# Expert slots cut into four quarters of 32 rows instead of two halves of 64

## The reference

```python
scores = sigmoid(x @ gate_w)                       # 1024 x 32 experts, in 4 groups
...                                                # two groups are barred, six experts per token are kept
g = ragged_dot(xs, w_gate, group_sizes)            # xs: 6144 rows (1024 tokens x 6), sorted by expert
u = ragged_dot(xs, w_up, group_sizes)              # w_gate, w_up: 32 x 256 x 176
d = ragged_dot(silu(g) * u, w_down, group_sizes)   # w_down: 32 x 176 x 256
expert_out = sum(d[unsort_idx].reshape(T, 6, 256) * weights[..., None], axis=1)
shared = (silu(x @ sw_gate) * (x @ sw_up)) @ sw_down
```

## Time and profile before

| | |
|---|---|
| median of 3 runs | 800.51 us (800.24 to 805.26) |
| the profiled execution | 803.87 us |
| its span on the core | 802.10 us, so 1.77 us lie around it |
| TensorE's granted clock, mean | 0.949 of full speed |

### The profile page before, as it was taken

The page is one execution under the profiler, slowest core; times in us unless marked ns, Lnnn a source line. Parts: engine busy times, 40 slices in busy tenths (PEclk is TensorE's granted clock), DMA queues, the critical chain, the costliest instruction groups (busy, mean ns, idle before and its releaser), DMA issues. The chain is left out here.

```text
span 802.1 us, 17814 instructions
## 1 busy us (share of the span) xinstructions
PE 712.0 (89%) x6749; PEld 447.1 (56%) x6749; DVE 447.9 (56%) x1151; ACT 305.7 (38%) x668; POOL 205.3 (26%) x263
## 2 busy tenths in 40 slices
PE   4999978876889999999999998699699999999945
PEld 3777755644344454665656775477445555555534
DVE  2567658876368887565645554259723443434426
ACT  1233334354310102444444443233255656556440
POOL 4000110143200000000000000024447777777422
PEclk9999999999779999999999999579879999999979
DMA  9500000000295000000000000195023232232157
GB/s 260 160 2 2 2 2 2 2 3 3 102 301 190 1 1 1 2 2 1 2 2 2 2 3 2 45 309 132 10 70 98 95 97 96 92 101 92 62 175 230
DMA packets 47544, 55.24 MB, mean 69 GB/s; under 512 B 6918, under 2 KB 42598, under 8 KB 46758
## 3 DMA queue, kind: packets, MB, share of 16 engines
q1 hardware_dynamic: 40390, 36.86, 15.8%
q0 software_dynamic: 6656, 16.85, 6.6%
q10 hardware_dynamic: 416, 0.39, 0.2%
HBM read 41.45 MB, written 12.65 MB: 67 GB/s over the span
## 5 line engine op out<-in xcount | busy, mean ns | idle before, releaser
L680 ACT ACTIVATE pt<-bank 128x512 f32<-128x512 f32 x192 | 104.2, 595 | 201.1 <-PE bank L390 112.8
L378 PE MATMUL bank<-kk,qT 32*128 32x256 f32 x768 | 109.6, 402 | 12.3 <-DVE qs L836 9.6
L836 DVE TENSOR_REDUCE qs<-bank 128x4 f32<-128x512 f32 x128 | 82.3, 684 | 54.9 <-PE bank L378 54.8
L1123 POOL TENSOR_TENSOR rstd<-vare,half 128x1 f32<-128x1 f32 x32 | 18.4, 574 | 348.6 <-DVE vare L899 348.6
L378 PEld LDWEIGHTS bank<-kk,qT 32*128 32x128 f32 x768 | 67.4, 185 | 38.1 <-issue 28.8
L1599 PE MATMUL bank<-x_wgu,x_xgT 128*64 128x352 f32 x256 | 84.8, 476 | 0.0
L1599 PE MATMUL bank<-wgu,x_xgT 128*64 x256 | 84.8, 475 | 0.0
L390 PE MATMUL bank<-qT,kk 32*128 32x512 f32 x256 | 75.9, 670 | 1.7 <-ACT pt L680 1.1
L1565 POOL DMA_INDIRECT out_rows<-x_og,g_out_row x64 | 66.6, 1041 | 38.1 <-DVE x_og L1692 27.6
L1561 POOL DMA_INDIRECT x_xg<-x_rows,g_x_row x64 | 62.1, 971 | 26.5 <-issue 18.3
L1625 PE MATMUL bank<-x_wd,x_hT 88*64 88x256 f32 x256 | 61.9, 385 | 0.0
(11 more groups left out here) (252 smaller groups left out, 1370.0 us busy)
## 6 DMA issues: line engine op xcount, KB each, us to landing
g_y<-out_rows SPq DMA_DIRECT2D x16, 384.0 KB, 8.0
wgu<-in_L_ffn_w_gate SPq DMA_DIRECT2D x4, 1408.0 KB
wgu<-in_L_ffn_w_up SPq DMA_DIRECT2D x4, 1408.0 KB
wd<-in_L_ffn_w_down SPq DMA_DIRECT2D x32, 176.0 KB
sparse_table<-f_m_re SPq DMA_DIRECT2D x2, 1024.0 KB, 11.8
f_m_re<-sparse_table SPq DMA_DIRECT2D x2, 1024.0 KB, 6.0
f_idx_row<-in_L_ffn_mask_idx SPq DMA_DIRECT2D x1, 1024.0 KB
x_rows<-x_all SPq DMA_DIRECT2D x1, 1024.0 KB, 5.2
```

What stands on the lines that cost most here:

```text
L378: return pe.matmul(bank, q, k, start=first, stop=r == 1, skip_group_check=True)
L680: act.activation(T.pt[2 * (t % 2) + u][:, :], STB[u][:, :], ACT.Exp, scale=own[v].scale).then_inc(exp_done, 1)
L836: dve.tensor_reduce(T.qs[v % 3][:, g:g + 2, 32 * j + 16:32 * j + 18], SB[u][:, :].rearrange("p (g e k) -> p g e k", g=2, e=2), AX.X, ALU.m ...
```

## The change

`SHARE` becomes 4 and `SROWS` 32. The rounding of each expert's rows costs less, 223 sub-blocks are left, and the slots are 56 instead of 64, so 28 rounds instead of 32. In each slot, four quarters of 32 rows stand on 32 columns of the array each. One reads its weights in place; the other three need a copy. For gate and up, ACT copies quarter 1, DVE quarter 2, and an SP transfer from SBUF to SBUF quarter 3. For down, DVE copies quarters 1 and 2 and an SP transfer quarter 3. There are two buffers for each of these instead of four. `x_xgT` and `x_hT` have one buffer instead of two, `x_sil` two instead of four. The lists of ACT and DVE are put in another order. In `route`, the tables are 56 wide instead of 64, and the expert numbers are 224 instead of 128, which takes one more small instruction on DVE and one more on PE.

```diff
-SHARE = 2
+SHARE = 4
...
+        @block.sync
+        def _(sp):
+            def move_gate_up(q):
+                for n in slots(q):
+                    if n >= 2:
+                        sp.wait_ge(gu_done, n - 1)
+                    unit = unit_of(sp, n, 3)
+                    sp.dma_start(in_copy(X.wgu[n % 2][2][:]), in_wgu(unit)).then_inc(wgu_moved[n % 2], 16)
...
+            def move_down(q):
+                for n in slots(q):
+                    if n >= 2:
+                        sp.wait_ge(down_done, n - 1)
+                    unit = unit_of(sp, n, 3)
+                    sp.dma_start(in_copy(X.wd[n % 2][2][0:MH, :, :]), in_wd(unit)).then_inc(wd_moved[n % 2], 16)
...
+            for c in range(-2, ROUNDS):
+                move_gate_up(c + 2)
+                move_down(c)
...
-                    pe.wait_ge(wgu_ready, n + 1)
+                    pe.wait_ge(wgu_ready1, n + 1)
+                    pe.wait_ge(wgu_ready2, n + 1)
+                    pe.wait_ge(wgu_moved[n % 2], moved(n))
...
-                    pe.wait_ge(wd_ready, n + 1)
+                    pe.wait_ge(wd_ready, 2 * n + 2)
+                    pe.wait_ge(wd_moved[n % 2], moved(n))
...
+            def copy_gate_up(q, i):
+                for n in slots(q)[i:i + 1]:
+                    if n >= 2:
+                        dve.wait_ge(gu_done, n - 1)
+                    unit = unit_of(dve, n, 2)
+                    dve.tensor_copy(in_copy(X.wgu[n % 2][1][:]), in_wgu(unit)).then_inc(wgu_ready2, 1)
...
             for c in range(-2, ROUNDS + 2):
                 copy_out(c - 2)
-                copy_upper(c)
-                hidden(c + 1)
+                copy_down(c - 1)
+                for i in range(2):
+                    hidden(c + 1, i)
+                    copy_gate_up(c + 2, i)
```

More of the change, by code:

```diff
@@ L1455, in _ @@
             for i in range(GROUPS_OF_SUBS):
-                then(dve.tensor_scalar(G.passed[:, i, :], upto, T.row[:, 1:2], None, ALU.is_le))
+                then(dve.tensor_scalar(G.passed[:, i, :], upto, T.row[:, 1 + i:2 + i], None, ALU.is_le))
             then(dve.tensor_reduce(G.number[:], G.passed[:], AX.X, ALU.add))
@@ L1537, in experts @@
         out_ready = sem("out_ready")
-        wgu_ready = sem("wgu_ready")
+        wgu_ready1 = sem("wgu_ready1")
+        wgu_ready2 = sem("wgu_ready2")
+        wgu_moved = [sem(f"wgu_moved{i}") for i in range(2)]
         wd_ready = sem("wd_ready")
+        wd_moved = [sem(f"wd_moved{i}") for i in range(2)]
         scattered = [sem(f"scattered{i}") for i in range(4)]
@@ L1660, in silu @@
                     act.wait_ge(gu_done, n + 1)
-                    act.activation(X.sil[n % 4][:], gu[n % 4][:, 0:MI], ACT.Silu).then_inc(sil_ready, 1)
+                    if n >= 2:
+                        act.wait_ge(h_ready, n - 1)
+                    act.activation(X.sil[n % 2][:], gu[n % 4][:, 0:MI], ACT.Silu).then_inc(sil_ready, 1)
             def copy_hidden(q):
@@ L1868, in decoder @@
         T.x_all = keep("x_all", [128, B, D])
+        at_packed = keep.at
         T.packed = keep("packed", [128, 398])
@@ L1910, in decoder @@
         G.share = [keep(f"g_share{i}", [128, D]) for i in range(2)]
-        shared_to = keep.at
-        G.stats, G.mv = keep("g_stats", [128, B, 6]), keep("g_mv", [128, B, 2])
-        G.vare, G.rstd = keep("g_vare", [128, B]), keep("g_rstd", [128, B])
-        slot = Memory(nc, first, onehots_end)
+        slot, routing = Memory(nc, first, end - weights), Memory(nc, routing_at, routing_to)
         X.xg = [slot(f"x_xg{i}", [128, D]) for i in range(4)]
-        X.og, X.xgT = ([slot(f"x_{n}{i}", [128, 2, D]) for i in range(2)] for n in ("og", "xgT"))
+        X.og = [slot(f"x_og{i}", [128, 2, D]) for i in range(2)]
+        X.xgT, X.hT = slot("x_xgT", [128, 2, D]), slot("x_hT", [128, 2 * D])
+        X.h, X.sil = [slot(f"x_h{i}", [128, MI]) for i in range(4)], [routing(f"x_sil{i}", [128, MI]) for i in range(2)]
         shared_wgu, shared_wd = Memory(nc, end - weights, end - weights + 2 * KT * 2 * MI * 4), Memory(nc, end - 4 * D * 4, end)
-        X.wgu = [place(f"x_wgu{i}", [128, KT, 2 * MI]) for i, place in enumerate((slot, slot, shared_wgu, shared_wgu))]
-        scores, shares = Memory(nc, scores_at, scores_to), Memory(nc, shared_at, shared_to)
-        X.wd = [place(f"x_wd{i}", [128, 2, D]) for i, place in enumerate((shares, shares, shared_wd, shared_wd))]
-        X.hT, X.sil = [scores(f"x_hT{i}", [128, 2 * D]) for i in range(2)], [scores(f"x_sil{i}", [128, MI]) for i in range(4)]
-        X.h = [shares(f"x_h{i}", [128, MI]) for i in range(4)]
+        X.wgu = [[place(f"x_wgu{i}{s}", [128, KT, 2 * MI]) for s, place in ((1, slot), (2, slot), (3, shared_wgu))] for i in range(2)]
+        X.wd = [[place(f"x_wd{i}{s}", [128, 2, D]) for s, place in ((1, slot), (2, slot), (3, shared_wd))] for i in range(2)]
         last = Memory(nc, end - weights, end)
@@ L2003, in constants @@
             "rounds": rounds, "rope": rope,
-            "row": np.stack([np.arange(128), SROWS * np.arange(128)], 1).astype(np.float32), "columns": np.arange(128, dtype=np.float32),
+            "row": np.stack([np.arange(128)] + [SROWS * (128 * i + np.arange(128)) for i in range(GROUPS_OF_SUBS)], 1).astype(np.float32), "columns": np.arange(128, dtype=np.float32),
             "spare": (128.0 * (ENTRIES + 1 + np.arange(SLOTS))[None, :] + np.arange(128)[:, None]).astype(np.float32),
```

103 lines of the change are left out of this document (60 added, 43 removed).

## The result

The changed kernel takes 869.04 us (median of 5 runs, 865.5 to 880.88), the kernel before, run beside it, 804.18 (5 runs, 800.24 to 807.72): a ratio of 1.0832, with a 95% interval of 1.0791 to 1.0873. The forecast was 791 us.

What follows compares the result with a forecast made beforehand. PE's columns bound the expert stage at 5.55 us a round. Four rounds fewer (-22.2), 28 x 0.25 for nearness, 6 for fill and drain and -0.5 for route give -9.7 us: 791 us forecast, range 783 to 812.

Steps and rivals of the forecast that it cites:

- SP itself has 4 x (0.7 + 0.33) = 4.1 us: SP's list in an expert round: four register loads and transfer issues take 4.1 us, inside the round.
- if SP's register load takes over 1.3 us: Expert stage: one of three listed conditions under which the prediction would be wrong.
- 0.25 a round for their nearness: Expert rounds: resources so close that a round takes 5.80 us, not 5.55; charged as 28 x 0.25.
- Small waits: Rival, expert rounds: DVE copies slowed beside POOL or PE's loads uncovered, round 6.1, 799 us, no change; chance 0.24.
- fill and drain: Start and end of the expert stage: about 3 us each, 6 us in all, bounds 3 and 8.
- the 0.5 us forecast for `route`: In `route`: tables an eighth smaller save 0.8 us, less 0.3 for an added instruction and wider cast.
- Four quarters stream together: PE's expert matmuls run on four column tiles at once; the rival without this gave over 900 us, chance 0.02.
- PE's round of 5.55: Expert stage: PE never stops, so its streamed columns bound a round at 5.55 us, unchanged by sharing.
- The landing of 2.6 to 3.4: SP's gate-up quarter of 352 KB takes 2.6 to 3.4 us from issue to landing.
- The rival of late transfers: Expert stage: gate-up quarters landing after 4.5 us make the loop 6.5 us and bound the round; 810 us, chance 0.24.
- POOL is not locked out: Rival: float32 SBUF copies on DVE stop POOL writing descriptors; POOL's round 8.0 us, total 852 us, chance 0.04.
- the 95%: Expert stage: DMA engines go from 29% busy to some 95%, taking 5.3 us a round.

Runs made afterwards that it cites:

- e1: Changed kernel with SP's down transfer taken over by a copy on ACT: 823.79 us, ratio 1.026 to the kernel before.
- e2: Changed kernel with SP keeping the unit number loaded for gate-up and using it for down, transfers the same: 834.85 us, ratio 1.045 to the kernel before.
- e4: Changed kernel with no register loads on SP, its transfers taking fixed units: 832.60 us, ratio 1.038 to the kernel before.
- e8: Changed kernel with SP's transfers, and their loads, for the first two slots only; loads on PE, DVE and ACT stay: 800.73 us, ratio 1.000 to before.
- e7: Changed kernel with no unit-number loads on any engine, fixed units instead, all transfers kept: 805.43 us, ratio 1.004 to the kernel before.
- e12: Changed kernel with down quarter on ACT, 10 loads a round, no range tests, PE's loads behind gate-up, 16 more gathers: 811.58 us, ratio 1.011 to before.
- e9: Changed kernel with each engine loading a round's unit numbers in one instruction and keeping them for down: 834.92 us, ratio 1.040 to before.
- e3: Changed kernel with SP's down transfer moving 128 rows of gate-up weights instead of 88 down rows: 838.57 us, ratio 1.046 to before.

## Why the prediction was wrong

**The step that failed** is "SP itself has 4 x (0.7 + 0.33) = 4.1 us". The four took 8.11. The 0.33 was the issue of a store of 128 KB; these issues are 0.52 and 0.90. The 0.7 was the pace of loads on ACT and DVE where no transfer from SBUF to SBUF ran; here the loads alone are 0.27 to 1.27, with 0.18 of arithmetic and test behind each. SP thus became the bound, as the prediction's last sentence named it ("if SP's register load takes over 1.3 us"), but no rival carried it. e1, e2 and e4 show it: with SP freed of its down transfers, 44 us of the stretch come back, freed of the two loads for them 30, freed of all its loads 32.

**What the sum had no term for** is the effect of one resource on another. The prediction set loads, transfers and DVE's list side by side, each inside a round, and added 0.25 a round for their nearness. The runs give the excess over 142.9 us:

- loads on PE, DVE and ACT without transfers (e8): 10.0
- transfers without loads (e7): 17.8
- transfers with the loads on PE, DVE and ACT (e4): 41.9
- all of it, with SP's own loads (the changed kernel): 74.0

So 32 of the 74 are SP's own loads, which no run has without the transfers; they stand on one list with them. Another 14 (41.9 - 10.0 - 17.8) exist only where loads and transfers run together, a rough figure, as each stretch is of one execution. The transfers lengthen the loads (medians 0.30 to 0.5 on DVE and PE, e8 against e4), SP's loads delay the transfers, and PE waits for either. Which loads are hit depends on when they fall: in e1, where only gate-up transfers are left, DVE's median is 0.30 but PE's, at the head of a round, 0.58, and in e12, with PE's loads moved behind gate-up, PE's is 0.30 too. Taking loads away by engine, the excess falls from 74.0 to 41.9 (SP), 24.5 (DVE) and 17.8 (PE, ACT). After SP no single list is shown to be the bound.

**Small waits** were thus the right kind of rival for what SP's list leaves over, with too small a price (0.55 a round for the 41.9 us of e4, 1.6 a round); PE's loads, which it named, stand uncovered for 10.7 us in 15 rounds of the changed kernel. **The end** was charged as part of 6 us for fill and drain; the fill alone is 5.8 us longer, for 3 forecast, and the drain of POOL's queue, which no term of the sum held, adds 7.4. What the stages ahead gave back (3.3 us) is no gain of the change: the first gather of the changed kernel and its variants lies anywhere from 574.6 to 585.3 us, so the 0.5 us forecast for `route` can't be read either. In e8 the drain eats most of the saving: 22.2 - 10.0 - 7.3 (44.9 us behind its last `x_og`) - 5.3 (its first at 604.7, of which 1.5 is fill and 3.9 the stages ahead) is -0.4, and its span is 802.5 for 802.1.

**What held.** Four quarters stream together: in the changed kernel four matmuls of 32 columns start within 0.01 us and the next four 0.29 or 0.30 later.

```profile
702.89 0.46 PE L1647 MATMUL bank<-wgu,x_xgT 128*32 x1
702.90 0.47 PE L1647 MATMUL bank<-x_wgu,x_xgT 128*32 128x352 f32 x3
703.19 0.46 PE L1647 MATMUL bank<-wgu,x_xgT 128*32 x1
```

So PE's round of 5.55 was right as a bound (16 of e7's 27 rounds take 5.52 to 5.72). The landing of 2.6 to 3.4 held at 2.5 to 3.8. The rival of late transfers had the sign right, but not the mechanism: no landing of `x_wgu` that the trace shows takes over 3.8 us, short of its 4.15, and transfers were late because they were issued late. The copy of 704 columns on DVE, forecast 0.55, takes 0.53. POOL is not locked out: beside six DVE copies a round its gathers take 0.95 to 1.44 us, 0.99 in the median, where they took 0.94 to 1.04 before. So the full form of the rule quoted in the prediction (the Trainium skill, SBUF — State Buffer, section "SBUF: two separate sides") does not hold for them here. The DMA engines are at 61% for the 95%, since a round was half as long again; with rounds of 5.95 in the mean (e7) they are at 80%.

**In the reading of before** one thing was overlooked. The prediction calls the register load "not in the trace"; for SP that is so, but the view of the load's own line lists it for DVE, 0.30 us, with 0.19 and 0.02 behind it. Those would have split the 0.77 from copy to copy into what can be cut (tests, needless loads) and what can't, and shown the outliers of 0.55.

**What stays open.** Why a load is slower beside transfers within SBUF (whether it waits in a queue of its own engine or in SBUF) was not separated. POOL's drain is 1.85, 9.20, 2.09 and 6.58 us in four lists of indirect transfers: not SP, not loads, not the number alone; what in the order of them sets it is open. Whether the granted clock (0.85 to 0.95) costs anything of its own was not tried. From 620 to 740 PE is busy 6.5 us a round in the changed kernel (96.9 us in 15 rounds, clock 0.89) and 5.5 in e1 (104.0 in 19, clock 1.00). But SP's list fills the round there by itself, and e1 is slow at a clock of 1.00 all the same. Why the fill grew by 5.8 us was not looked into.

## What to carry to other kernels

Where a loop reads an address from memory into a register on every engine, that read is a term of each engine's list, with all that the call puts behind it (here 0.30 + 0.21 us), and it must be priced beside the traffic that the change adds: here the loads of PE, DVE and ACT cost 10 us alone (e8) and 24 beside the transfers (e4 over e7), and SP's four a round 32 more. Before a copy is handed to an idle queue, write that queue's list out in full, issue by issue and in the shape it will have, and look at what is at its head: an engine with nothing to do may still need longer for four instructions than the bound engine for a round. And when a change takes rounds away, look at what is paid once at the stage's end, since it may move too.

## What was not expected of the hardware

- A load of one number from SBUF into a register takes 0.27 us on SP and 0.30 on DVE and PE at rest, and up to 1.52 on SP, 1.21 on DVE and 1.09 on PE in kernels with transfers within SBUF. In one instruction, each further number adds about 0.23 us (e9).
- Issuing a transfer of 88 rows takes SP 0.90 us, one of 128 rows 0.49 to 0.52, and the load behind it 1.26 us in the median behind 88 rows and 0.28 behind 128. In e3, with 128 rows in all four, the loads' median on SP is 0.33, with 88 in two of them 0.54.
- The drain of POOL's queue at a stage's end is the same to the nanosecond, 9196 ns, in twelve kernels with the same list of indirect transfers, whatever else ran, and 1846, 2091 and 6582 in the three with other lists.
